# Four graph layers on one core: mixing by quarters of the array, a plain step order in layer 1, wide groups in layer 2

## The reference

```python
# layer 0: graph convolution, attention over neighbours, MLP
xp = einsum('mn,bnf->bmf', L_norm, x)          # L_norm = 2 adj / lam_max - I
x1 = relu(layernorm(xp @ Wc + bc)) + x
...                                            # 4-head attention, MLP, two more layernorms
# layer 1: two graph convolutions, then LSTMs over windows of 1..4 nodes
h = relu(einsum('ts,bsh->bth', adj, x @ Wg0 + bg0))
h = relu(einsum('ts,bsh->bth', adj, h @ Wg1 + bg1))
...                                            # four LSTMs overwrite h in turn
# layer 2: mixing, product, batch norm, relu, product, batch norm
agg = einsum('nm,bmd->bnd', A_hat, x)          # A_hat = adj + I, scaled by degrees
h = relu(batchnorm(agg @ W1.T + b1))
out = batchnorm(h @ W2.T + b2)                 # statistics over all 8192 rows
# layer 3: one-head attention, then a refinement by the children's sum
refined = attn_out @ Wo + bo + x
child_sum = einsum('nm,bmd->bnd', adj, refined)
out = refined + gamma * (child_sum - refined) * is_parent
```

## Time and profile before

| | |
|---|---|
| median of 3 runs | 2340.16 us (2339.61 to 2341.25) |
| the profiled execution | 2342.6 us, span 2340.7 us |
| PE busy | 2172.1 us, 93% of the span |
| DVE busy | 1391.9 us, 59% |
| ACT busy | 1206.5 us, 52% |
| POOL busy | 480.1 us, 21% |

### The profile page before, as it was taken

How to read it: one execution, slowest core, us unless ns; L and a number is a source line. 1 busy time by engine, 2 the same in 40 slices (tenths; PEclk the granted TensorE clock), 3 DMA queues, 4 the chain that set the end, 5 groups by cost and what they waited for, 6 DMA issues and landing times. The chain is left out here.

```text
span 2340.7 us, 39332 instructions
## 1 busy us (share of the span) xinstructions
PE 2172.1 (93%) x14671; PEld 1939.7 (83%) x14671; DVE 1391.9 (59%) x2733; ACT 1206.5 (52%) x2295; POOL 480.1 (21%) x905
## 2 busy tenths in 40 slices
PE   5999999999969989999999999999998897979997
PEld 3888888888859988888888889988887897968886
DVE  3788778877855645443334433444433787857776
ACT  1453455345523347644444434444433566958887
POOL 3344334433430000000000000000000221016665
PEclk9999999999979999999999999999999898989999
DMA  2110111011122101000000000000000331012221
GB/s 97 33 55 18 40 49 54 18 40 49 37 82 63 54 30 36 1 18 1 1 1 19 19 1 1 1 1 1 1 1 18 107 109 54 0 32 64 72 72 50
DMA packets 76397, 81.77 MB, mean 35 GB/s; under 512 B 6545, under 2 KB 74001, under 8 KB 75409
## 3 DMA queue, kind: packets, MB, share of 16 engines
q1 hardware_dynamic: 76304, 80.51, 10.9%
HBM read 55.33 MB, written 25.17 MB: 34 GB/s over the span
## 5 line engine op out<-in xcount | busy, mean ns | idle before, releaser
L298 PE MATMUL ps<-R 128*128 128x256 f32 (+3 forms) x8520 | 1490.9, 335 | 38.2 <-DVE R L1506 14.2
L298 PEld LDWEIGHTS ps<-R 128*128 128x128 f32 x8520 | 1326.6, 190 | 183.2 <-DVE R L767 14.8
L1200 ACT ACTIVATE late_half<-ps,lstm_bias 128x512 f32<-128x512 f32 (+2 forms) x460 | 283.0, 669 | 383.0 <-PE ps L298 382.9
L340 POOL TENSOR_TENSOR ln_veps<-ln_mv,eps_tile 128x2 f32<-128x2 f32 x128 | 28.4, 222 | 1283.0 <-DVE ln_mv L323 1283.0
L829 PE MATMUL ps<-H 128*128 128x256 f32 x1024 | 237.6, 381 | 3.0 <-ACT H L750 1.7
L829 PEld LDWEIGHTS ps<-H 128*128 128x128 f32 x1024 | 189.0, 191 | 26.1 <-ACT H L750 1.9
L1235 DVE TENSOR_TENSOR late_half<-late_half 128x1024 f32<-128x1024 f32 (+2 forms) x32 | 37.6, 1175 | 186.8 <-ACT late_half L1200 186.8
L1197 ACT ACTIVATE late_half<-late_half 128x1024 f32<-128x1024 f32 (+2 forms) x66 | 68.1, 1031 | 124.4 <-DVE late_half L1240 78.4
L1237 DVE TENSOR_TENSOR late_half<-late_half 128x1024 f32<-128x1024 f32 (+2 forms) x32 | 37.6, 1175 | 132.6 <-ACT late_half L1200 132.6
L366 DVE SCALAR_TENSOR_TENSOR H<-H,ln_rstd 128x256 f32<-128x256 f32 x192 | 106.5, 596 | 6.7 <-POOL ln_rstd L333 3.2
L319 DVE BATCH_NORM_STATS2 ln_stats<-H 128x6 f32<-128x256 f32 x256 | 95.9, 416 | 5.3 <-POOL H L711 2.0
(11 more groups left out here) (208 smaller groups left out, 2860.6 us busy)
## 6 DMA issues: line engine op xcount, KB each, us to landing
H<-in_x SPq DMA_DIRECT2D x64, 256.0 KB, 4.1
...
```

Of the source, the lines that this page charges most:

```text
L298: mm = pe.matmul(out, lhsT(a), rhs(b), start=start and n == 0, stop=stop and n == len(PASSES) - 1)
L1200: ins = act.activation(into[q][:, m, 0:x.cols], gate_ps(q, m, x.cols), ACT.Tanh if q == TANH_G else ACT.Sigmoid, bias=lstm_bias[:, x.p - 1 ...
```

## The change

There are four parts.

**1. Mixing on quarters of the array.** Each 128 x 128 x 128 matmul of a mixing becomes four of 64 x 64 x 64, one for each graph g (rows 0 to 63 or 64 to 127 of the array) and each half c of 64 features (columns), without the zero blocks. A group takes 16 small matmuls. Graph g's result goes to bank g of the stream, so a mixing now uses both banks, and its readers on ACT and DVE see it in another order (`mixed_by_graph`, `graph_order`).

```diff
+    def mixed_by_graph(s):
+
+        return ps[:, BANKS * s:BANKS * (s + 1), 0:KD * P].rearrange("p g (c i) -> p g c i", i=NODES)
+
+    def graph_order(v):
+
+        return v.rearrange("p k (n g i) -> p g (k n) i", n=TILES, g=2)
...
+    def mix_by_graph(pe, s, src, weights):
+
+
+        alone(pe, waits_passed)
+        for k in range(KD):
+            for n in range(TILES):
+                for c in range(2):
+                    for g in range(2):
+                        f = k * P + NODES * c
+                        mm = pe.matmul(mixed_by_graph(s)[part_of(c), g, TILES * k + n, :],
+                                       src[part_of(g), n, f:f + NODES], weights[part_of(g), part_of(g)],
+                                       start=True, stop=True)
+        return mm
+
...
                     pe.wait_ge(xs_loaded[s], 16 * turn + 16)
                     pe.wait_ge(var2_ready[s], 2 * turn + 1)
-                    for n in range(TILES):
-                        for k in range(KD):
-                            mm = pe.matmul(feature_major(s, 0)[:, k, n * P:(n + 1) * P],
-                                           xs_t[s][:, n, k * P:(k + 1) * P], lnormT[:], start=True, stop=True)
-                    mm.then_inc(mixed[s], 1)
+                    mix_by_graph(pe, s, xs_t[s], lnormT).then_inc(mixed[s], 1)
                 if slot == 1:
```

```diff
+            for s in ORDER:
                 sp.dma_start(xg_t[s], rows_of_group(state0, s, 0)).then_inc(xg_loaded[s], 16)
             sp.dma_start(wstage[1], t["whh"][1]).then_inc(stage_loaded[1], 16)
...
+            with sp.Fori(0, TURNS - 1) as turn:
+                for s in ORDER:
                     sp.wait_ge(ga_done[s], turn + 1)
                     sp.dma_start(xg_t[s], rows_of_group(state0, s, turn + 1)).then_inc(xg_loaded[s], 16)
...
+                    act.activation(graph_order(zg[s][:, 0]), mixed_by_graph(s), ACT.Copy).then_inc(zg_hi[s], 1)
+                for s in ORDER:
                     act.wait_ge(tg_ready[s], KD * turn + KD)
                     act.activation(h1[s][:, 0], tg_f[s], ACT.Relu).then_inc(h1_hi[s], 1)
-                if slot == 4:
+                for s in ORDER:
                     act.wait_ge(gb_done[s], turn + 1)
...
+                    for k in range(KD):
+                        ins = act.activation(columns_of(Hflat, s, turn)[:, k, :].rearrange("p (n g i) -> p g n i",
+                                                                                           n=TILES, g=2),
+                                             mixed_by_graph(s)[:, :, TILES * k:TILES * k + TILES, :], ACT.Relu)
+                    ins.then_inc(gcn_ready[s], 1)
...
+            with dve.Fori(0, TURNS) as turn:
+                for s in ORDER:
+                    split_mixed(s, turn)
+                add_mixed_bias(3, turn)
+                add_mixed_bias(2, turn)
+                split_hidden(3, turn)
+                add_mixed_bias(1, turn)
+                split_hidden(2, turn)
+                add_mixed_bias(0, turn)
+                split_hidden(1, turn)
+                add_row_bias(3, turn)
+                split_hidden(0, turn)
+                for s in ORDER[1:]:
+                    add_row_bias(s, turn)
 
         @block.tensor
         def _(pe):
             pe.wait_ge(wg_ready, 1)
...
+            with pe.Fori(0, TURNS) as turn:
+                for s in ORDER:
...
-                if slot == 1:
+                    pe.wait_ge(gcn_ready[s], turn + 1)
+                    mix_by_graph(pe, s, xg_t[s], adjT).then_inc(ga_done[s], 1)
+                for s in ORDER:
                     pe.wait_ge(zg_ready[s], turn + 1)
...
-                if slot == 4:
+                for s in ORDER:
                     pe.wait_ge(ug_ready[s], turn + 2)
-                    mix(feature_major(s, 1), ug_t[s]).then_inc(gb_done[s], 1)
-
-            weave(pe, TURNS, plan1, "pe", stage)
+                    mix_by_graph(pe, s, ug_t[s], adjT).then_inc(gb_done[s], 1)
```

```diff
+            def relu(g):
+                b = g % BUFS
+                for h in range(2):
+                    if nth(g):
+                        act.wait_ge(split_half[b], 2 * nth(g) - 1 + h)
+                    for m in range(KH * h, KH * h + KH):
...
-                        ins = act.activation(rf32[s][:, m, :], columns_of(state, s, turn)[:, m % KD, :], ACT.Relu,
+                        ins = act.activation(rf32[b][:, m, :], wide_cols(state, g)[:, m % KD, :], ACT.Relu,
                                              bias=bn1_ss[:, 1, m:m + 1], scale=bn1_ss[:, 0, m:m + 1])
-                    ins.then_inc(r_ready[s], 1)
...
+                    ins.then_inc(relu_half[b], 1)
+
+            def evict(g):
+                b = g % BUFS
+                act.wait_ge(relu_half[b], 2 * nth(g) + 2)
+                act.wait_ge(read_half[b], 2 * nth(g) + 2)
+                act.activation(wide_cols(Hflat, g), wide_out(g), ACT.Copy).then_inc(out2_ready[b], 1)
+
+            for g in range(BUFS):
+                relu(g)
+            for g in range(WIDES):
+                if g + BUFS < WIDES:
+                    relu(g + BUFS)
+                evict(g)
...
+                b = g % BUFS
+                c = chains[b]
+                for h in range(2):
+                    k = slice(KH * h, KH * h + KH)
+                    dve.wait_ge(relu_half[b], 2 * nth(g) + h + 1)
+                    if nth(g):
+                        dve.wait_ge(read_half[b], 2 * nth(g) - 1 + h)
+                    c.step(dve.tensor_scalar(rr[b][:, 0, k, :], rf32[b][:, k, :], 1.0, None, ALU.mult))
                     c.settle()
-                    dve.tensor_tensor(rr[s][:, 1], rf32[s], raw(rr[s][:, 0]), ALU.subtract).then_inc(r_split[s], 1)
-                if slot == 3:
-                    dve.wait_ge(out2_ready[s], turn + 2)
...
+            def stats(g):
+                b = g % BUFS
+                dve.wait_ge(out2_ready[b], nth(g) + 1)
+                for m in range(KD):
+                    dve.bn_stats(bn_stats2[:, m, 6 * g:6 * g + 6],
+                                 wide_cols(Hflat, g)[:, m, :]).then_inc(st2_taken[b], 1)
+
+            for g in range(BUFS):
+                split(g)
+            for g in range(WIDES):
+                if g + BUFS < WIDES:
+                    split(g + BUFS)
+                stats(g)
...
+            for g in range(WIDES):
+                b = g % BUFS
+                if g >= 8 // KD:
+                    pe.wait_ge(out2_ready[b], nth(g - 8 // KD) + 1)
+                for h in range(2):
+                    pe.wait_ge(split_half[b], 2 * nth(g) + h + 1)
                     for m in range(KD):
-                        for k in range(MB):
-                            mm = exact_mm(pe, feature_major(s, 0)[:, m, :],
+                        for k in range(KH * h, KH * h + KH):
+                            mm = exact_mm(pe, wide_out(g)[:, m, :],
                                           lambda q: l2w2_r[:, q, k, m * P:(m + 1) * P],
-                                          lambda q: rr[s][:, q, k, :], k == 0, k == MB - 1)
-                    mm.then_inc(dn2_done[s], 1)
-
-            weave(pe, TURNS, plan3, "pe", stage)
+                                          lambda q: rr[b][:, q, k, :], k == 0, k == MB - 1)
+                    mm.then_inc(read_half[b], 1)
```

```diff
             link(pool.tensor_scalar(rest_gamma[:], parent_gamma[:], -1.0, 1.0, ALU.mult, ALU.add))
+            link(pool.tensor_scalar(refine, adj_bd, parent_gamma[:, 0:1], None, ALU.mult))
+            link(pool.tensor_scalar(own_row, ident[:], rest_gamma[:, 0:1], None, ALU.mult))
...
+            dve.wait_ge(refine_turned, 1)
+            link(dve.tensor_copy(refineT[:], ps0(5)[:, 0:P]))
...
+            pe.transpose(ps0(5)[:, 0:P], refine, ident[:]).then_inc(refine_turned, 1)
             pe.wait_ge(p_ready, SQUARINGS + 1)
...
-        act={0: 8, 2: 27, 3: 29, 4: 34, 5: 38, 7: 38, 9: 43, 10: 45, 11: 48, 13: 57},
+        act={0: 8, 2: 27, 3: 29, 4: 34, 5: 38, 7: 38, 9: 43, 10: 45, 13: 57},
         dve={1: 23, 6: 35, 8: 42, 11: 47, 12: 51},
-        pool={1: 23, 3: 28, 11: 48, 12: 51},
+        pool={1: 23, 3: 28, 12: 51},
         sp={10: 33, 13: 57})
...
                 if slot == 12:
                     dve.wait_ge(child_done[s], turn + 1)
-                    dve.wait_ge(rest_ready[s], turn + 1)
-                    c.step(dve.scalar_tensor_tensor(out=y3_t[s], in0=token_major(s, 1), scalar=parent_gamma[:, 0:1],
-                                                    in1=x3b_t[s], op0=ALU.mult, op1=ALU.add))
+                    c.step(dve.tensor_tensor(y3_t[s], token_major(s, 1), x3_t[s], ALU.add))
...
                     pe.wait_ge(rf_ready[s], turn + 2)
                     for n in range(TILES):
```

178 lines of the change are left out of this document (63 added, 115 removed).

## The result

The changed kernel takes **2304.07 us** (median of 4 runs, 2298.93 to 2308.27) against 2339.89 for the kernel before on the same chip (2339.42 to 2341.25); the ratio is 0.9845 with a 95% interval of 0.9819 to 0.9871. Forecast: 2302, range 2288 to 2322. Two of the four runs took 2308 us and two 2299 to 2300; one of the two long ones had a mean granted clock of 0.931, the other three 0.975 to 0.980. The profiled execution took 2300.29 us with a span of 2298.5, the one of before 2342.6 and 2340.7: 42.2 us less span, where the sum of my terms had 38.2.

What follows compares the result with a forecast made beforehand. PE was taken to bound the kernel, apart from its waits and the untouched LSTMs. Terms -4.4 - 4.4 - 17.3 - 6.2 - 6.2 + 0.3 = -38.2 us gave 2302 us, range 2288 to 2322.

Steps and rivals of the forecast that it cites:

- the main term: Layer 1: a turn falls from 18.66 to 16.5 us with small mixings, over eight turns -17.3 us.
- The crossing of a turn: Layer 1, from a turn's start to its first product: ACT's evictions and high part set it, 4.9 us.
- the step that failed: Layer 0: 32 mixings each 0.23 us cheaper, at most 7.4 us, of which 60% shows: -4.4 us.
- My own condition for being wrong: Layer 1 gaining under 10 us, the quoted layer 0 case, or DVE without gaps in layer 2's second part.
- Layer 2, first part: 32 small mixings gain 0.23 us each, of which 60% shows: -4.4 us, between 0 and -12.
- the 60%: Layers 0 and 2's first part: share of 32 x 0.23 us expected to show, the rest turning into longer waits.
- Layer 2, second part: Wide groups: 384 matmuls of 512 columns replace 768 of 256; with start, end and aggregations -6.2 us.
- Layer 3: Refinement: ACT loses an instruction, PE's wait for q and k's eviction goes, the end shortens: -6.2 us.
- The term "5.1 us": Layer 3: PE's wait for ACT's eviction of q and k, 4.6 us in 180, over some 200 us; expected to go.
- Rival 1: Small matmuls don't overlap, each mixing costs 0.81 to 0.88 us, parts 1 and 2 give nothing: 2328 us; chance 0.06.
- Rival 2: Layer 1 shows its chains: turn 19.3 us, layer 5 us longer, 2319 us; chance 0.12.
- Rival 3: PE's clock falls in layer 1, up to 8.2 us a turn, 2367 us; chance 0.04.

Runs made afterwards that it cites:

- doubling run: The changed kernel with each small mixing of layer 0 issued twice in a row; 2314.22 us, ratio 0.9894.
- `l1_small_woven`: The changed kernel with layer 1 in the woven order of before but with small mixings; 2330.47 us, ratio 0.9955.

## Why the forecast held

- **The order of size and the main term.** Layer 1 was forecast at -17.3 and gave -20.0. The price of a small mixing inside a row of them was 0.47 and is 0.53. The crossing of a turn was put at 4.9 us and is 4.5 (744.88 - 740.41), because PSUM evictions of 256 columns follow each other at 0.27 us and not at their busy time of 0.37. "layer 1's turn is 16.5 us with one gap, ahead of the first product" was wrong in its second half: ACT doesn't set this stretch, the mixings do. With it falls my remark that 0.58 per mixing would cost the same; PE is full there, so a longer mixing should show in full (not tested).
- **Layer 0, the step that failed.** "Part of each gain turns into a longer wait at L852 or at a product. I take 60%": -4.4 forecast, -0.2 measured, and when the part stood alone -0.6 us between the medians, with an interval of -3.5 to +0.7. The term was mis-sized in its share, not in its price (0.62 against 0.58 us). The wait for L802, in the kernel before L767 with 11.4 us from 100 to 660 us, was not among the rows that I chose. It takes the gain in full where the mixing stands ahead of it, and in the doubling run it took 10.2 of 16 us. About 1 us is left of the gain, and the falls of the clock hid that. I had read the list of waits for its largest entry, L784, and not for which wait ends next behind each mixing. My own condition for being wrong, "if PE in layer 0 is less busy by the whole 7 us while the layer is as long as before", didn't come, since the clock's falls filled what was freed; the layer was as long as before all the same.
- **Layer 2, first part.** -4.4 forecast and -5.2 measured agree by accident. The turns show 1.2; 2.4 is a load that was slow in the one profile of before; the rest fits the 3.7 us more of low clock at its start (17.5 against 13.8). So here too the 60% was wrong: 1.2 us are left of 32 x 0.23 = 7.4, and in the kernel's time (2300.2 with full mixings, 2301.28 and 2304.07 with small ones) nothing shows. The wait "right ahead of the mixing" depends on ACT and DVE more than on PE: it grew from 0.9 to 1.3 us.
- **Layer 2, second part.** -6.2 forecast, -4.7 by the profiles and 5.1 when undone. Start (-0.6), end (+0.7) and aggregation (-0.8) came as worked out. One price was off: 0.226 us per matmul instead of 0.2247 is 0.5 us over 384. The rest is the start at the lower clock level: the first 52 matmuls take 14.64 us where 52 x 0.226 = 11.75, which is 2.9 lost, against 4.85 - 26 x 0.1196 = 1.7 before. That is not a price of the wide groups, as the profiles of both widths show (above): with the clock low for equally long the part gives 5.6 us.
- **Layer 3.** -6.2 forecast, -8.5 by the profiles, 7.1 to 8.8 when undone. The mechanism was right and the end gave its 1.0 (2298.5 - 2289.52 = 8.98 us from L1716 on, where the earlier trace rows gives 2340.7 - 2330.74 = 9.96). The term "5.1 us" was mis-sized: I took the waits as the list has them, 0.25 each, and one costs 0.40 us from one stream's products to the next. "PE is at 97%, so no more can come" was wrong with it: PE is busy 173.67 of 180 us from 2110 to 2290 in the kernel before, but behind a wait its instructions overlap less (0.69 us from start to start above in place of 0.19), so the busy share hides a part of what a wait costs.
- **The gap ahead of layer 1** (-4.0) I had set to 0: "the first loads ... I leave as it is". I had not asked which stream PE begins with and when its load is issued, though the plan's leads say it.
- **The rivals.** Rival 1 fell: 128 small stationary operands a turn overlap. Rival 2, that layer 1 shows its chains, doesn't hold in the plain order; something like it happens in the woven one, where it costs 9 us and not 5. Its time was added up wrongly: -21 us are the other terms alone, and with the 5 us by which layer 1 would be longer it is 2324 us and not 2319, so the range up to 2322 left it out. By the Trainium skill, "TensorEngine Tiling (Array Packing)", section PSUM Bottleneck, the copies out of PSUM may bound once tiling has made the products shorter. The trace of `l1_small_woven` agrees in part: PE waits 2.54 us for them in the turn shown, but the same copies hold up nothing in the plain order, so it is where they stand and not how long they take. Rival 3, the fall of the clock in layer 1, didn't come in the plain order, and came in six of eight turns in the woven one: about 1.2 us for the products of a turn, not the 8.2 that I had priced for all 96.
- **By luck.** Two terms too large (layer 0 and the wide groups, 5.7 us) and two too small with one forgotten (layers 1 and 3, the gap, 9.0 us) cancel in the main. By the medians, 35.8 and 38.1 us below before, the sum of 38.2 looks better still, and that is luck too.
